# One pass over an audio tower layer: the FFN's layer norm moved from DVE to ACT, its transposes moved behind the token probabilities, and the orders around them

## What is computed

```python
h = tok(x, Wq, bq, Wkv, bkv)             # 16 tokens mixed into 8, softmax over 8x8, per block
h = h + attn(layernorm(h), Wq, Wk, Wv, Wo)   # 12 heads, 3 key/value heads, rope, softmax
h = h + ffn(layernorm(h), w_in, b_in, w_out) # gelu(hn @ w_in.T + b_in) @ w_out, 768 hidden

def layernorm(x, eps=1e-05):
    m = mean(x); v = var(x)
    return (x - m) / sqrt(v + eps)
```

## Time and profile before

| | us |
|---|---|
| median of 3 runs | 1128.8 (1128.35 to 1129.33) |
| the profiled execution | 1131.78 |
| its span in the trace | 1130.0 |
| PE busy | 1005.1 (89%) |
| DVE busy | 829.2 (73%) |
| ACT busy | 728.2 (64%) |
| POOL busy | 437.4 (39%) |

### The profile page before, as it was taken

How to read it: one execution, slowest core, us unless ns; L and a number is a source line. 1 busy time by engine, 2 the same in 40 slices (tenths; PEclk the granted TensorE clock), 3 DMA queues, 4 the chain that set the end, 5 groups by cost and what they waited for, 6 DMA issues and landing times. The chain is left out here.

```text
span 1130.0 us, 24498 instructions
## 1 busy us (share of the span) xinstructions
PE 1005.1 (89%) x7232; PEld 867.8 (77%) x7232; DVE 829.2 (73%) x2095; ACT 728.2 (64%) x2530; POOL 437.4 (39%) x583
## 2 busy tenths in 40 slices
PE   3788999999999999999999999999999999999876
PEld 2567878787877888787778878788878778887865
DVE  2677777777777787787778778777778777878751
ACT  2455666677676677667667766666766766776651
POOL 0333434443444343343444344434334343433430
PEclk7798999999999999999999999999999999999999
DMA  5233434333433433343443344344334334333331
GB/s 162 66 97 101 128 106 121 121 109 101 134 114 106 130 115 103 118 128 109 118 121 109 110 127 122 100 130 122 102 108 132 109 114 126 112 110 118 109 105 38
DMA packets 139936, 127.49 MB, mean 113 GB/s; under 512 B 30993, under 2 KB 123025, under 8 KB 139921
## 3 DMA queue, kind: packets, MB, share of 16 engines
q1 hardware_dynamic: 137632, 124.16, 37.0%
q10 hardware_dynamic: 2288, 3.15, 0.8%
HBM read 70.63 MB, written 56.62 MB: 113 GB/s over the span
## 5 line engine op out<-in xcount | busy, mean ns | idle before, releaser
L300 ACT ACTIVATE E<-ring,m_neg 128x128 f32<-128x128 f32 x768 | 271.3, 388 | 75.2 <-DVE m_neg L511 75.1
L400 POOL TENSOR_TENSOR E<-E,e_rcp 128x512 f32<-128x512 f32 x192 | 198.4, 1040 | 289.4 <-DVE e_rcp L531 286.3
L511 DVE TENSOR_REDUCE m_neg<-ring 128x4 f32<-128x512 f32 x192 | 122.6, 681 | 103.9 <-PE ring L707 103.9
L392 POOL TENSOR_TENSOR q_tok<-rot_c,rot_s 128x384 f32<-128x384 f32 x128 | 126.5, 999 | 149.2 <-DVE rot_s L489 149.2
L300 ACT ACTIVATION_READ_ACCUMULATOR E<-ring,m_neg 128x1 f32 x768 | 174.2, 227 | 0.0
L707 PEld LDWEIGHTS ring<-qkT 64*128 64x128 f32 x1536 | 93.0, 192 | 77.1 <-ACT qkT L294 76.6
L707 PE MATMUL ring<-qkT 64*128 64x128 f32 x1536 | 105.4, 285 | 52.0 <-ACT qkT L294 52.0
L522 DVE STREAM_TRANSPOSE EB<-E 128x512 f32<-128x512 f32 x192 | 134.3, 700 | 17.7 <-POOL E L400 17.7
L831 PE MATMUL ring<-wo_sb,OT 128*128 128x192 f32 x768 | 141.8, 336 | 0.7 <-ACT OT L308 0.7
L694 PE MATMUL bank<-wout_sb,G 128*128 128x192 f32 x768 | 135.4, 326 | 2.9 <-ACT G L366 2.9
L831 PEld LDWEIGHTS ring<-wo_sb,OT 128*128 128x128 f32 x768 | 126.4, 194 | 2.8 <-issue 2.2
(11 more groups left out here) (122 smaller groups left out, 2413.3 us busy)
## 6 DMA issues: line engine op xcount, KB each, us to landing
spill<-EB SPq DMA_DIRECT2D x64, 512.0 KB, 2.6
ET<-spill SPq DMA_DIRECT2D x256, 128.0 KB, 2.7
spill<-EB SPq DMA_DIRECT2D x64, 256.0 KB, 2.8
ET<-spill SPq DMA_DIRECT2D x256, 64.0 KB, 2.0
x_sb<-in_x_dram SPq DMA_DIRECT2D x64, 192.0 KB, 2.5
out_dram<-out_sb SPq DMA_DIRECT2D x64, 96.0 KB, 2.3
x_sb<-in_x_dram SPq DMA_DIRECT2D x64, 64.0 KB, 2.4
w_raw<-in_w_att_dram ACTq DMA_DIRECT2D x2, 576.0 KB, 5.1
```

The lines of the kernel that those rows point to most:

```text
L300: last = nc.scalar.activation(E[:, a, s * P:(s + 1) * P], RING[a][:, s * P:(s + 1) * P], ACT.Exp, bias=m_neg[:, a, s:s + 1], accum_out=e_s ...
L392: nc.gpsimd.tensor_tensor(q_tok[:, a, c], rot_c[:, a, c], rot_s[:, a, c], ALU.add).then_inc(q_out, 1)
L400: nc.gpsimd.tensor_tensor(e, e, r, ALU.mult).then_inc(prob_out, 1)
L511: nc.vector.tensor_reduce(m_neg[:, a, REP * g:REP * (g + 1)], RING[a][:, 512 * g:512 * (g + 1)].rearrange("p (h k) -> p h k", k=P), AX_X, ...
```

## The change

The norm's second step, (h - mean) * rs, becomes one scale and one bias on ACT: rs * h + off, where off = -mean * rs is a new operation of POOL behind the power (`off2`, semaphore `ln2_off`). ACT's `normalised(0)` stands at the beginning of a step ahead of the first `qkT` copies, `normalised(1)` between the token probabilities `t_a` and the copy of `t_aT`. DVE's two `normalise` calls are gone; `attention_added` now also waits for `hn_out`, since ACT reads `h2`. On POOL `rstd2` of a = 0 stands ahead of `turned_in(0)`. On DVE both query banks of a = 1 are rotated before the block transpose of the last group. On PE `hn_turned` stands behind `tok_probs_turned`, and `tok_h` between the query tiles and the key tiles. On SP both spills are issued before the fills.

```diff
@@ SP
                     sp.wait_ge(blocks_out, 6 * q + 3 * a + 2 + k)
                     need(sp, filled[k], 64 * (2 * (q - 1) + a + 1))
                     sp.dma_start(spill[a, :, c], EB[:, a, c]).then_inc(spilled[k], 16)
+                for k, (s0, heads) in enumerate(PIECES):
+                    c = slice(s0 * P, (s0 + heads) * P)
                     need(sp, pv_mm, 4 * (q - 1) + 2 * a + k + 1)
                     sp.wait_ge(spilled[k], 16 * (2 * q + a + 1))
@@ ACT
+                def normalised(a):
+                    act.wait_ge(ln2_off, 2 * (p - 1) + a + 1)
+                    need(act, hT_mm, p - 1)
+                    scale, bias = rs2[:, a:a + 1], off2[:, a:a + 1]
+                    nc.scalar.activation(hn[:, a, 0:D], h2[:, a, :], ACT.Identity, scale=scale, bias=bias)
+                    nc.scalar.activation(hn[:, a, D:DP], h2[:, a, P:D], ACT.Identity, scale=scale,
+                                         bias=bias).then_inc(hn_out, 1)
...
+                if ffn:
+                    normalised(0)
+                if att:
                     qk_turned(0)
...
                         nc.scalar.activation(t_a[:, a, :], t_e[:, a, :], ACT.Copy,
                                              scale=t_rs[:, a:a + 1]).then_inc(t_norm, 1)
+                if ffn:
+                    normalised(1)
+                if tok:
                     act.wait_ge(aT_mm, n + 1)
@@ POOL
                     nc.gpsimd.tensor_tensor(rs2[:, a:a + 1], ve2[:, a:a + 1], half_neg[:, 0:1],
                                             ALU.pow).then_inc(ln2_rs, 1)
+                    wait_apart(pool, pool_passed, (ln2_rs, done))
+                    nc.gpsimd.tensor_scalar(off2[:, a:a + 1], mv2[:, a, 0:1], rs2[:, a:a + 1], -1.0,
+                                            ALU.mult, ALU.mult).then_inc(ln2_off, 1)
...
+                if ffn:
+                    rstd2(2 * p - 1, 0)
                 if att:
                     turned_in(0)
-                if ffn:
-                    rstd2(2 * p - 1, 0)
-                if att:
                     for g in range(NKV):
@@ DVE
                     dve.wait_ge(y_mm, done)
+                    need(dve, hn_out, done - 2)
...
-                if ffn:
-                    dve.wait_ge(ln2_rs, 2 * p - 1)
-                    need(dve, hT_mm, p - 1)
-                    normalise(h2, mv2, rs2, hn, 0).then_inc(hn_out, 1)
...
-                    rotate(1, (0,))
+                    rotate(1, (0, 1))
                     blocks_turned(0, 2, p)
-                    rotate(1, (1, 2))
+                    rotate(1, (2,))
                     keys_added(1)
-                if ffn:
-                    dve.wait_ge(ln2_rs, 2 * p)
-                    normalise(h2, mv2, rs2, hn, 1).then_inc(hn_out, 1)
@@ PE
                     tok_probs_turned()
+                if ffn:
+                    hn_turned()
                 if att:
-                    qk_turned(1)
+                    qk_turned(1, range(6))
                 if tok:
                     tok_h()
-                if ffn:
-                    hn_turned()
+                if att:
+                    qk_turned(1, (6, 7))
                 if att:
                     scores(1)
```

More of the change, by code:

```diff
@@ L144, in program @@
         st2, mv2, ve2, rs2 = sb("st2", [P, 2, 6]), sb("mv2", [P, 2, 2]), sb("ve2", [P, 2]), sb("rs2", [P, 2])
-        hn = sb("hn", [P, 2, DP])
+        hn, off2 = sb("hn", [P, 2, DP]), sb("off2", [P, 2])
         HH, HL = sb("HH", [P, 2, 2, P], F32R), sb("HL", [P, 2, 2, P], F32R)
@@ L178, in program @@
         y_mm, h2_out, h2_copied = sem("y_mm"), sem("h2_out"), sem("h2_copied")
-        ln2_st, ln2_mv, ln2_ve, ln2_rs, hn_out = (
-            sem(n) for n in ("ln2_st", "ln2_mv", "ln2_ve", "ln2_rs", "hn_out"))
+        ln2_st, ln2_mv, ln2_ve, ln2_rs, ln2_off, hn_out = (
+            sem(n) for n in ("ln2_st", "ln2_mv", "ln2_ve", "ln2_rs", "ln2_off", "hn_out"))
         hT_mm, HH_out, HL_out = sem("hT_mm"), sem("HH_out"), sem("HL_out")
@@ L400, in probs @@
                     nc.gpsimd.tensor_tensor(e, e, r, ALU.mult).then_inc(prob_out, 1)
-                if att:
-                    turned_in(0)
                 if ffn:
@@ L406, in step @@
                 if att:
+                    turned_in(0)
                     for g in range(NKV):
@@ L677, in qkv, with qk_turned @@
                                (x2h, W2S[:, c]), (x2l, W2S[:, c]))).then_inc(qkv_mm, 1)
-                def qk_turned(a):
-                    for t in range(8):
+                def qk_turned(a, tiles=range(8)):
+                    for t in tiles:
                         if t in (0, 3):
```

## The result

The changed kernel takes 1060.36 us (median of 4 runs, 1059.65 to 1062.17), the kernel before beside it 1128.57 us (4 runs, 1127.98 to 1129.33). The ratio is 0.9394, with a 95% interval of 0.9383 to 0.9406. The forecast was 1056 us, 4.4 too low. The profiled execution took 1060.68 us.

A forecast was written before the change was run, and what follows sets the result against it. PE's queue, its work and waits, bounds the kernel (busy 1005.1 of 1130.0 us). Loop 65, start 4 and end 3.5 make 72.5 from 1131.8: 1059, less 3.0 to the median, 1056 us; range 1046 to 1079.

The forecast's parts named there:

- The scores' wait: PE, mid-step: 1.65 us before the scores because ACT copies `HH`, which waits for `hn`, ahead of the `qkT` copies.
- The query wait: PE, mid-step: 0.73 us before the second three query tiles, from DVE's block transpose between the two query banks.
- 2.1 us a step: Loop: scores start at 589.9 to 590.05 instead of 592.10; 31 x 2.1 = 65 us.
- `hn` has 0.4 us to spare: ACT to PE: `hn` written at 586.5 to 586.6, before PE asks for it at 587.04, so no wait.
- rival A: PE at `hn_turned`: `hn` is late, PE waits 0.3 to 0.9 us each step, 1075 us; chance 10%.
- DVE's reserve is 0.4 us: DVE before `key_max`: it can come 2.5 us sooner, against 2.1 needed.
- rival B: DVE becomes the bound: `key_max` is late, only 1.5 us a step won, 1075 to 1080 us; chance 9%.
- A key operation gets 0.3 us shorter: DVE's key additions beside POOL: with POOL's `q_tok` half 0.4 us sooner, one may shorten, keys 0.3 us sooner.
- 2.2 us a step: Loop: the gain if the keys come 0.3 us sooner, with PE arriving at the key tiles at 588.80.
- SP: nothing in the loop, 7.5 us with the clock at the ends: Both spills before the fills: nothing in the loop, 4 us at the start, 3.5 at the end.
- From the profiled execution to the median: Whole kernel: the median of the runs is 3.0 us below the profiled execution, taking 1059 to 1056 us.
- C: Before the scores: the wait only changes its owner, nothing is won, 1129 us; chance 4%.
- D: ACT: `normalised(0)` ahead of the first `qkT` copies waits for a late -mean * rs; slower, 1149 us at 4.5 us; chance 4%.

The follow-up runs named there:

- the first experiment: The kernel before with one edit: ACT copies `HH` behind both `qkT` copies, norm on DVE and PE's order kept; 1075.13 us, ratio 0.9525.
- the best kernel: The changed kernel with `tok_h` behind the key tiles, all eight query and key tiles turned directly behind `hn`; 1051.07 us, ratio 0.9309.

## Why the prediction held

- **The scores' wait is an order on ACT, 1.65 us a step.** Right. Three runs show it: ACT's order alone takes it away, PE's old order brings it back, DVE's order alone leaves it as it is. The earlier trace rows had shown ACT idle 2.87 us for `HH` with two copies queued behind.
- **The query wait is DVE's order.** Right, 12 to 16 us by the two runs with and without it. It isn't quite gone: the fourth query tile still waits 0.2 us, because `q_tok`'s second half, put at 587.8 in the replay, comes 0.1 us later behind `off2` and PE goes on 0.06 us after it. The prediction let such a tenth disappear in the key tiles' wait for `k_tok`; that wait isn't there, so it counts in full. As an estimate, `off2` ahead of `q_tok` costs up to 31 x 0.2 = 6 us; no run has the norm on ACT without it or with `q_tok` first.
- **2.1 us a step, scores 2.86 to 3.01 us behind the first tile.** 2.02 in 28 like steps, and 3.01, the late end. The loop gave 62.6 us, not 65. The ends gave 8.7 where the sum had 7.5, in part by the clock; so the two misses cancel in half, and the total is nearer than its terms.
- **`hn` has 0.4 us to spare.** Wrong in size, 0.11 to 0.15. Two terms were too small, and PE comes 0.11 us sooner after POOL's power (521.05 less 519.51, for 587.04 less 585.39). The gap ahead of POOL's new operation was put at 0.08 us and is 0.21. ACT's pair was put at 0.8 us and takes 0.88 (520.02 to 520.90); the bound of 1.14 held, and the Trainium skill (ScalarE: Activation LUTs, What ACT_TABLE_LOAD costs), by whose figures the pair was an estimated 0.86 us, was nearer than my value. So rival A was closer than 0.4 us made it look, though it would have been cheap: `hn` later by 0.45 us cost 0.19 us a step at the scores.
- **POOL's new operation costs 0.25 us.** 0.26.
- **DVE's reserve is 0.4 us.** It still idles 0.90 us before the maxima; rival B didn't come. In the first experiment, where DVE keeps the norm and the scores come as early, it has no idle time there left.
- **A key operation gets 0.3 us shorter.** The first did, from 0.59 to 0.29 us; the second stays at 0.59 (0.58 in the earlier trace rows), because POOL's copy to `h_cur` lies beside it, as before. The keys are done 0.29 us sooner behind the first tile of `t_a` (522.58 less 520.83, for 588.86 less 586.82), as the prediction had it. But PE gets to the key tiles only at 523.01, 0.43 us after that, since `q_tok` has held it up. So the 2.2 us a step didn't come, and not for want of the keys.
- **SP: nothing in the loop, 7.5 us with the clock at the ends.** The two runs with and without SP's order differ by 6 to 7 us, and their traces show 4.6 to 4.9 of them at the end, more than my 3.5, and 0 and 1.9 in the loop. For the start my 4 is not shown: 4.5 us came in the profiled executions, but with SP's old order in the changed kernel none of it was lost. At the end `hn` did cost what was taken off for it: PE's wait for it in the last pair grew from 0.94 to 1.68 us, 0.7 for my 0.5.
- **From the profiled execution to the median.** Here lie about 3 of the 4.4 us. The sum from the profiled execution was 1059.3, and it measured 1060.7, 1.4 off. But the kernel before was profiled in an execution 3.0 us above its median, and I carried that over. After, the profiled execution is 0.3 us above its median. Executions of the kernel before differ by as much: of nine, those with a mean granted clock of 0.977 or 0.978 took 1129.8 to 1131.6 us, two with 0.985 1127.0. A profiled execution that is slower than its runs says nothing on the next one.
- Rivals C and D: the steps shrank to 31.27 us, the 31.2 of the forecast, and ACT waits 1.80 us before the first `qkT` copies where it waited 2.57, less by the pair's cost; `normalised(0)` delays nothing. D's 1149 us has a slip in it: by its own terms 4.5 us give 1056 + 2.7 x 31, about 1140.

What stays open: whether `hn` sooner (without POOL's extra operation) would give more in the best kernel, and whether `q_tok`'s first half ahead of `off2` would take away the fourth tile's 0.2 us; neither was tried.

## What to carry to other kernels

When an engine waits for a copy whose source has long been there, look at what stands ahead of that copy in the copying engine's queue: one order changed there, or the order of what it waits for, was worth 46 to 53 of 68 us, while the moved arithmetic was worth 17, each measured with the other parts in place, so that they don't add up. The same remedy is worth nothing a second time, so each is to be measured in the kernel in which it is to live. And before an operation is put earlier on DVE, see what POOL does at that time: its end, not the place in the queue, may set when the result is there.

## What the runs showed of the hardware

- **Some DVE operations on SBUF data end with POOL's.** `k_tok` (128x128, two inputs in SBUF) takes 0.28 us alone; started while POOL formed `q_tok` it took 0.86 us, and `hn` (128x64, one input with per-row scalars) 0.99 us instead of 0.30. Both ended 0.06 to 0.14 us after POOL's operation. The same holds in every step of the kernels before and after for `xn`, the first layer norm's operation of 128x192 with one input: 0.37 us alone, 1.22 beside POOL's `E` product of 1.04 us, 0.12 us after its end. It looks less like a slower rate than like a wait for the end of one operation of POOL: `hn`'s first operation (128x192), which started 0.2 us ahead of the end of `q_tok`'s first half, kept its 0.37 us. In the same stretch the block transposes (0.70 us) and the products that read PSUM (0.54 us) kept their times. The Trainium skill (GPSIMD Engine Reference, Key points) names contention on the shared SBUF interfaces for DVE instructions with two SBUF inputs or in a 2-port performance mode; the trace agrees for `k_tok`, and which mode `hn` runs in no run shows.
- **The gap between two dependent operations of POOL** was 0.21 us ahead of `off2`, where the gap ahead of the power was 0.08 us (518.94 less 518.64 + 0.22). Ahead of `off2` stands a wait with an increment of its own (`wait_apart`), ahead of the power a plain wait; whether that or the operation before it makes the difference no run shows.
